# The running sum of squares of a gated feed-forward stage, added up by GpSimd in place of VectorE

## The reference, cut to what matters

```python
def _L0_ffn_ref(x, w_gate_up, w_proj):       # x: LayerNorm of (16, 100, 512)
    wq_gu = ternary_quant(w_gate_up)          # (2 * 2048, 512)
    gate, up = jnp.split(jnp.einsum('bsd,hd->bsh', x, wq_gu), 2, axis=-1)
    h = jax.nn.silu(gate) * up                # 2048 hidden columns
    hn = h * rsqrt(mean(h * h, axis=-1, keepdims=True) + eps)
    return jnp.einsum('bsh,dh->bsd', hn, ternary_quant(w_proj))
```

## Time and profile before

| what | value |
|---|---|
| three runs | 1809.84, 1813.79, 1816.64 us; median 1813.79 |
| the profiled execution: its time | 1811.94 us |
| its span | 1810.0 us (1.9 us of the time lie around it) |
| mean granted TensorE clock | 0.948 |
| busy over the span | PE 1608.7 (89%), DVE 1178.9 (65%), ACT 1033.9 (57%), POOL 669.5 (37%) |
| the changed stage | about 679.8 to 997 us of the span |

### The profile page before, as it was taken

The page is one execution under the profiler, slowest core; times in us unless marked ns, Lnnn a source line. Parts: engine busy times, 40 slices in busy tenths (PEclk is TensorE's granted clock), DMA queues, the critical chain, the costliest instruction groups (busy, mean ns, idle before and its releaser), DMA issues. The chain is left out here.

```text
span 1810.0 us, 35818 instructions
## 1 busy us (share of the span) xinstructions
PE 1608.7 (89%) x11995; PEld 998.3 (55%) x11995; DVE 1178.9 (65%) x2637; ACT 1033.9 (57%) x2563; POOL 669.5 (37%) x529
## 2 busy tenths in 40 slices
PE   4788999999999989989999777776499999999997
PEld 3655656656656555545555444555356666666664
DVE  4866796797787787786887777676833333333334
ACT  2447746746746737565665686663745555555554
POOL 4613323323423420000000122232167777777774
PEclk8789999999999999999999999886699999999999
DMA  8820130130130139786777200011446657656626
GB/s 264 287 101 10 36 94 13 36 97 10 37 96 10 53 119 348 232 300 214 252 233 239 93 2 29 29 38 55 127 102 152 154 140 166 147 134 149 149 45 218
DMA packets 145061, 226.58 MB, mean 125 GB/s; under 512 B 38049, under 2 KB 93601, under 8 KB 144760
## 3 DMA queue, kind: packets, MB, share of 16 engines
q1 hardware_dynamic: 108888, 195.90, 34.1%
q0 software_dynamic: 29344, 21.29, 7.2%
q10 hardware_dynamic: 6656, 7.11, 1.1%
HBM read 175.00 MB, written 98.80 MB: 151 GB/s over the span
## 5 line engine op out<-in xcount | busy, mean ns | idle before, releaser
L2792 PE MATMUL g_ps<-ring,xT 128*128 x1572 | 300.0, 326 | 1.5 <-issue 0.8
L2741 POOL DMA_INDIRECT acc<-rows,slot_sources x131 | 208.8, 1594 | 104.9 <-issue 55.2
L1070 POOL TENSOR_TENSOR pr<-pr,sm 128x1444 f32<-128x1444 f32 (+1 forms) x64 | 137.3, 2145 | 215.7 <-DVE sm L1108 215.7
L2899 DVE SCALAR_TENSOR_TENSOR hf<-sg,g_ps 128x192 f32<-128x192 f32 x131 | 46.4, 354 | 237.1 <-ACT sg L2848 237.1
L2792 PEld LDWEIGHTS g_ps<-ring,xT 128*128 128x128 f16 x1572 | 141.4, 98 | 73.1 <-issue 7.6
L2731 POOL DMA_INDIRECT xg<-xtab,slot_sources x131 | 138.4, 1057 | 74.3 <-issue 72.5
L2814 PE MATMUL d_ps<-ring,hT 128*128 x655 | 162.8, 379 | 0.7 <-ACT hT L2861 0.7
L1102 DVE TENSOR_REDUCE sm<-s_banks 128x2 f32<-128x722 f32 (+2 forms) x128 | 97.5, 762 | 67.1 <-PE s_banks L835 64.6
L990 ACT ACTIVATE pr<-s_banks,sm 128x361 f32<-128x361 f32 (+1 forms) x208 | 115.3, 563 | 30.7 <-DVE sm L1102 29.2
L892 PE MATMUL o_bank<-cT,N_hi 128*128 128x400 f16 x512 | 128.4, 332 | 0.0
L835 PE MATMUL s_banks<-kvp,qp 128*128 128x361 f16 (+1 forms) x624 | 116.9, 318 | 10.7 <-ACT pr L990 6.1
(11 more groups left out here) (335 smaller groups left out, 3909.1 us busy)
## 6 DMA issues: line engine op xcount, KB each, us to landing
split_f<-in_gu SPq DMA_DIRECT2D x64, 384.0 KB, 4.2
split_gu<-split_o SPq DMA_DIRECT2D x64, 384.0 KB, 3.0
ring<-split_gu SPq DMA_DIRECT2D x32, 768.0 KB
head<-in_head SPq DMA_DIRECT2D x16, 864.0 KB, 9.3
tern_w<-in_tern SPq DMA_DIRECT2D x48, 256.0 KB
split_f<-in_down SPq DMA_DIRECT2D x32, 384.0 KB, 4.2
split_d<-split_o SPq DMA_DIRECT2D x32, 384.0 KB, 3.6
ring<-split_d SPq DMA_DIRECT2D x32, 256.0 KB
```

Of the source, the lines that this page charges most:

```text
L1070: nc.gpsimd.tensor_tensor(pr[:, s % 3, 0:n], pr[:, s % 3, 0:n], small[:, s % 3, 2, 0:n].unsqueeze(2).to_broadcast([P, n, KEYS]), ALU.mult) ...
L2741: nc.gpsimd.indirect_dma_start(out=core.acc[i % NACC][:, :], out_offset=bass.IndirectOffsetOnAxis(ap=core.sources[:, i:i + 1], axis=0), in ...
L2792: last = nc.tensor.matmul(g_ps[i % 2][:, 0:2 * INTER], xT[:, i % 2, a * KT + k, :], ring(i, (2 * k + w) * 2 * INTER, 2 * INTER), start=((k ...
```

## The change

A GpSimd block is added to the stage, which runs `add_square` for all steps in order, with the same waits as before. VectorE's `add_square` and its call in pass t go. Nothing else is altered: the buffers, the semaphores and the waits of ScalarE and TensorE on `summed` stay.

```diff
+            @block.gpsimd
+            def _(pool):
+                def add_square(c, t):
+                    n = c * HT + t
+                    pool.wait_ge(squared.sem, squared.after(n))
+                    if t:
+                        pool.wait_ge(summed.sem, summed.after(n - 1))
+                        nc.gpsimd.tensor_tensor(tot, tot, sq[:, t % 2, :], ALU.add
+                                                ).then_inc(summed.sem, 1)
+                    else:
+                        pool.sem_inc(summed.sem, 1)
+
+                for c in range(NCH):
+                    for t in range(HT):
+                        add_square(c, t)
+
             @block.vector
...
-                def add_square(c, t):
-                    n = c * HT + t
-                    dve.wait_ge(squared.sem, squared.after(n))
-                    if t:
-                        dve.wait_ge(summed.sem, summed.after(n - 1))
-                        nc.vector.tensor_tensor(tot, tot, sq[:, t % 2, :], ALU.add
-                                                ).then_inc(summed.sem, 1)
-                    else:
-                        dve.sem_inc(summed.sem, 1)
...
                             for j in STEP_SPLITS[t - 1]:
                                 es.lo(dve, c, j)
-                            add_square(c, t - 1)
```

## The result

The changed kernel took 1819.87 us (median of 10 runs, 1813.91 to 1829.15) against 1812.0 us for the kernel before (10 runs): ratio 1.0049, 95% interval 1.0032 to 1.0065, so some 8 us slower. A second comparison gave 1.0032 (1.0014 to 1.0051). The forecast was 1817 us in a range of 1803 to 1829; it put the change at 3.1 us, on top of the 1813.79 us of the first three runs of the kernel before.

What follows compares the result with a forecast made beforehand. TensorE was taken as the bound, VectorE the runner-up. Chunk terms 0.4 + 0.9 + 2.3 - 0.5 = +3.1 us took the profiled 1811.94 to 1815.0; with 1.85 carried over to the median, 1817 us, range 1803 to 1829.

Steps and rivals of the forecast that it cites:

- the bound of the gain: Most that VectorE's relief could bring TensorE: 8.1 us at chunk ends plus 2.9 before the root less 1.0: 10.0 us.
- The sum: Net effect over chunks 0 to 3: 0.4 + 0.9 + 2.3 - 0.5 = +3.1 us, slower.
- GpSimd's price by slope: Duration of one GpSimd add of 400 elements, from its instructions of 384 and 192: 1.03 us.
- The block of 0.83 us: Time one GpSimd add shuts out VectorE's low, splits or normalisation: 0.83 us, 0.34 if the product follows.
- Where the adds fall: Placing each add beside VectorE's instructions, pass by pass: +2.3 us for a chunk with LayerNorm work.
- The early claim: VectorE claims its turn at the shared ports while its instruction before still runs, so low goes ahead of the add.
- The statistics of pass 2: In chunk 2 the add of step 2 comes under these and holds up nothing.
- the wait for the sum in chunk 3: At the end of chunk 3, TensorE's 1.84 us wait for the last add would be gone: -1.84 us.
- the two blocks in passes 5 and 6: Two blocks of 0.83 us there against two removed adds: +0.68 us.
- B: Slower rival: every add cuts into a run of splits, 0.83 us each: +14.4 us, 1828 us; chance 0.22.
- C: Faster rival: VectorE keeps its claim through a run, adds fit into products, statistics and gaps: 1804 us at best; chance 0.20.
- D: No-change rival: TensorE's 2.71 us pace hides both the adds' removal and their blocks: 1814 us; chance 0.18.

Runs made afterwards that it cites:

- the two chosen adds: The kernel before with only the adds of steps 2 and 15 of each chunk on GpSimd, the latter behind the splits except in chunk 3: 1808.96 us, ratio 0.9986.
- Both: The kernel before with VectorE's adds kept, plus GpSimd adding two spare tiles at the same moments, for which nobody waits: 1849.37 us, ratio 1.0187.
- Half: The changed kernel with GpSimd adding only 200 of the 400 columns: 1802.58 us, ratio 0.9935 to the kernel before.
- Copy: The changed kernel with GpSimd copying the squares over the sum instead of adding them: 1802.36 us in a single execution.

## Why the prediction was right

**What bounds the kernel, and the bound of the gain.** TensorE's waits for VectorE were the right place to look. With every add gone the idle time fell by 8.7 us, against the bound of 10.0. As a bound on the time, 10.0 was wrong: the stage gained 16.9 us, because TensorE's busy time fell by 8.2 as well, 5.2 of them by the clock (estimate above). The sum had no term for the clock.

**The price of an add.** GpSimd's price by slope, 1.03 us, was its duration in most adds (1.03 to 1.06; median 1.04). The block of 0.83 us was right: two adds on one run of splits in chunk 2 made 3.63 us out of 1.96 (two times 0.84), L230 was held for 0.84.

**Where the adds fall.** The step came out right in sum and failed in its places. The forecast came to about 9.2 us of blocks in a chunk with LayerNorm work (0.61 an add); the trace has 36.6 us in four chunks (0.61 an add). That the two figures are the same is partly luck, since the second includes chunk 0, which had some 10 us of them, against 8 to 9 in each of the others. But I had low already claimed when an add came during the product, and normalised rows as the usual victims. In fact the add got in front of low (low's mean from 0.57 to 0.81 us), and the normalised rows were not held at all. For 0.83 us it is the same whether low or a piece of a split waits, so the error did not reach the sum. The early claim, read from one row, is not a rule. By the Trainium skill (SBUF — State Buffer, SBUF: two separate sides) the first to start gets the ports. Most adds of the changed kernel agree (849.88 above), and none of them took longer than 1.40 us; the add at 968.10 with the two chosen adds, which waited 1.9 us behind a run of five VectorE instructions, does not, and neither do the long waits in Both, Half and Copy.

**The sum.** The forecast was +3.1 us of waits; TensorE's idle time in the stage rose by 3.5 (29.3 against 25.8, means of three). Part of that closeness is luck, because errors cancel between the chunks. From one chunk's first gate matmul to the next one's, idle time changed by +1.5, +0.6, +1.6 and -0.2 us in chunks 0 to 3, against a forecast of +0.4, +0.9, +2.3 and -0.5. Busy time added 1.9 us, giving 5.4 in the stage; it is 3.5 us of clock, for which the sum had no term, less 1.6. The whole change was two to three times the forecast: 7.9 us between the medians of the first comparison and some 6 by the ratio of the second. The intervals reach down to 5.8 and 2.5 us, so the stage accounts for the second and falls just short of the first. The statistics of pass 2 covered an add, as said; the wait for the sum in chunk 3 went from 1.84 to 0.4 us, as said. The waits at the chunk ends did not shrink below 2 us, as said (2.67, 2.24 and 2.52 us in chunks 0, 1 and 2 against 1.46, 2.42 and 2.42); chunk 0's grew by 1.2 us where I had put 0.4. For the normalised row after pass 5 TensorE waited 2.61 us in each of chunks 1 to 3, at most 1.43 before: the two blocks in passes 5 and 6.

**The rivals.** B, every add cutting into a run, needed a mean block of 0.83 us; it was 0.61. C fell with the splits' and low's durations; its mechanism, VectorE keeping its claim through a run, did not occur in the changed kernel, but did in other kernels here. D fell too: the experiment with idle GpSimd work shows that TensorE's pace doesn't cover such blocks.

## What to carry to other kernels

Moving elementwise work from VectorE to GpSimd is not a relief as long as VectorE's other instructions read two SBUF tensors (or normalise SBUF to SBUF): a GpSimd instruction can hold them up for nearly its whole length (0.84 of 1.03 us), here 0.61 us in the mean against 0.49 us saved. Price the move by what VectorE does during GpSimd's instruction, and put it beside instructions that were not held up here (a PSUM input, the statistics) and that last as long as it does, or in idle stretches. Eight adds, most of them so placed, shortened the stage by 5 us where sixty lengthened it by 5; sixty held back to the product, which is half as long as an add, only broke even on VectorE. Where TensorE is near its full pace, a wait taken away can also bring back clock, so that a bound from waits alone is too low.

## What the runs showed of the hardware that was not expected

The granted clock: in this stage the time at half clock was 16 to 23 us before, 23 to 32 after, 6 to 11 without adds and 38 with GpSimd's spare adds, roughly following how much TensorE waited in it (25 to 27, 28 to 31, 17 to 18 and 53 us). For the same 1748 matmuls TensorE's busy time ran from 287.0 to 306.3 us.

Which engine goes first is not settled. An add that started 0.40 us after low (862.40, changed kernel) got in ahead of the splits and took 1.05 us; one that started 0.41 us after low (968.10, two chosen adds) waited out all four pieces and took 2.91. The same add in the second profile of that kernel (971.81) started 0.47 us after low, got in ahead and took 1.02 us. Long waits are no rare accident: three of 60 in Both, ten of 60 in Half and twelve of 60 in Copy, but none of 60 in each of the three profiles of the changed kernel. What decides between the two outcomes was not found.
